# Attention and ternary FFN on one core: the output projection's first tile joins the list between the score rounds, and VectorE masks three of four short rounds

## The reference, cut to what matters

```
xn = layernorm(x)
q, k, v = heads(xn @ Wq.T), heads(xn @ Wk.T), heads(xn @ Wv.T)
q, k = rope(q), rope(k)
attn = softmax(where(causal, q @ k.T / sqrt(32), -inf))
s = (attn @ v) @ Wo.T
h = gelu(layer_norm_quant(xn) @ ternary(w_fc).T)          # 2048 wide
g = silu(layer_norm_quant(h) @ ternary(w_proj).T)
out = x + s * g
```

## Time and profile before

| | us |
|---|---|
| median of 3 runs | 1092.42 |
| lowest and highest run | 1091.6, 1092.45 |
| the profiled execution | 1090.23 |
| its span, first to last instruction | 1088.5 |
| TensorE busy in it | 1062.7 |
| VectorE, ScalarE, GpSimd busy in it | 851.3, 771.9, 551.8 |

### The profile page before, as it was taken

How to read it: one execution, slowest core, us unless ns; L and a number is a source line. 1 busy time by engine, 2 the same in 40 slices (tenths; PEclk the granted TensorE clock), 3 DMA queues, 4 the chain that set the end, 5 groups by cost and what they waited for, 6 DMA issues and landing times.

```text
span 1088.5 us, 19703 instructions
## 1 busy us (share of the span) xinstructions
PE 1062.7 (98%) x7132; PEld 595.4 (55%) x7132; DVE 851.3 (78%) x1751; ACT 771.9 (71%) x1486; POOL 551.8 (51%) x1035
## 2 busy tenths in 40 slices
PE   4999999999999999999999999999999999999998
PEld 3565664448544584446734476444854458444673
DVE  7996877898758986689757997589875898668965
ACT  4797993589826887279853798358982688727984
POOL 2045471565715656265643766156571565626553
PEclk9999999999999999999999999999999999999999
DMA  9493005920129102571027610293012910256101
GB/s 328 166 104 92 1 14 90 118 84 21 38 52 155 40 3 40 80 124 40 4 40 100 104 40 15 57 106 89 22 38 51 156 40 3 40 82 84 40 20 61
DMA packets 87554, 75.66 MB, mean 70 GB/s; under 512 B 44705, under 2 KB 69281, under 8 KB 86945
## 3 DMA queue, kind: packets, MB, share of 16 engines
q1 hardware_dynamic: 87456, 74.41, 37.3%
HBM read 31.98 MB, written 8.40 MB: 37 GB/s over the span
## 4 chain that ended last, share of the span: by engine, by line
PE 80%; ACT 8%; DMA 4%; POOL 4%; DVE 2%; issue 1%; SPq 1%; POOLq 0%; DVEq 0%
PE banks L464 20%; PE banks L601 20%; PE banks L642 16%; PE banks L721 5%; PE banks L481 5%; PE banks L576 4%; PE banks L702 4%; ACT arena L931 3%; DMA norm_row<-norm_c 2%; POOL arena L1500 2%; PE banks L580 2%; ACT banks L911 2%; DMA arena<-in_L_ffn_w_proj_dram 1%; PE banks L587 1%; PE banks L498 1%
## 5 line engine op out<-in xcount | busy, mean ns | idle before, releaser
L911 ACT ACTIVATE banks<-banks,mix,scl 128x384 f32<-128x384 f32 (+2 forms) x384 | 248.6, 650 | 11.8 <-POOL mix L1473 6.1
L642 PE MATMUL banks<-proj_ones,arena 128*128 128x257 f16 (+1 forms) x1792 | 241.7, 272 | 0.0
L601 PE MATMUL banks<-xT,fcT 128*128 128x512 f16 x1024 | 227.7, 379 | 1.9 <-ACT xh_buf L869 1.4
L642 PEld LDWEIGHTS banks<-proj_ones,arena 128*128 128x128 f16 x1792 | 172.9, 97 | 42.3
L1421 POOL TENSOR_TENSOR xh_buf<-xh_buf 128x512 f32<-128x512 f32 x120 | 152.6, 1271 | 66.8 <-ACT xh_buf L869 65.6
L931 ACT ACTIVATE arena<-banks,scl 128x1280 f32<-128x1280 f32 x128 | 163.0, 1331 | 13.2 <-PE banks L702 9.6
L464 PE MATMUL banks<-xT,qkT 128*128 128x512 f16 x768 | 168.1, 379 | 0.1
L601 PEld LDWEIGHTS banks<-xT,fcT 128*128 128x128 f16 x1024 | 99.0, 98 | 122.6 <-ACT xh_buf L869 5.9
L1415 POOL TENSOR_TENSOR xh_buf<-xr_buf,xh_buf 128x512 f16<-128x512 f32 x32 | 36.9, 1175 | 208.8 <-ACT xh_buf L841 208.8
L1211 DVE CUSTOM_DVE_ANT_0 banks<-banks,mask_row 128x512 f32<-128x512 f32 (+1 forms) x224 | 137.7, 632 | 4.3 <-PE banks L576 2.6
L1473 POOL TENSOR_SCALAR mix<-mix,scl 128x1 f32<-128x1 f32 (+1 forms) x288 | 77.1, 268 | 125.8 <-DVE mix L1211 84.6
(11 more groups left out here) (181 smaller groups left out, 1469.2 us busy)
## 6 DMA issues: line engine op xcount, KB each, us to landing
stacks<-xh_buf SPq DMA_DIRECT2D x96, 128.0 KB, 5.5
stacks<-split_buf SPq DMA_DIRECT2D x96, 128.0 KB, 7.9
out_dram<-arena SPq DMA_DIRECT2D x32, 256.0 KB, 2.0
xr_buf<-in_L_attn_x_dram SPq DMA_DIRECT2D x7, 1024.0 KB, 10.1
resid<-in_L_attn_x_dram SPq DMA_DIRECT2D x28, 256.0 KB, 5.3
stacks<-in_L_ffn_w_fc_dram SPq DMA_DIRECT2D x1, 4096.0 KB, 25.7
arena<-in_L_ffn_w_proj_dram SPq DMA_DIRECT2D x1, 4096.0 KB, 15.7
mix<-norm_row SPq DMA_DIRECT2D x8, 256.0 KB, 5.1
```

What stands on the lines that cost most here:

```text
L601: mm = pe.matmul(banks[:, UP_BANKS[f % NUB], :], fcT[:, c, f * P:(f + 1) * P], xT[:, part, c, :], start=(c == 0 and part == 0), stop=(c == ...
L642: mm = pe.matmul(banks[:, DOWN_BANKS[h], 0:cols.stop - cols.start], hid[:, part, f, t * P:(t + 1) * P], proj_ones[:, f, cols], start=(f == ...
L911: mm = nc.scalar.activation(block, block, ACT.Exp, scale=col(EXP_SCALE), bias=exp_bias[:, i, h0 + k:h0 + k + 1], accum_out=row_sum[:, i, h ...
```

## The change

- `OUT_EARLY` goes: all four tiles of the output projection are entries of the running list, 48 instead of 36. `out_projection(b - 1)` ahead of the up-projection goes, and with it the scaling behind chunk 3 and the addition of x there; tile 0 is scaled and added as the others are, at rounds from `SCALED_AFTER`.
- `GIVEN` is planned for 144 entries instead of 132. After rounds 0 to 4 it stays at 0, 4, 12, 17, 20; after round 15 it is 55 instead of 51, after round 26 90 instead of 83, after round 38 128 instead of 118. `SCALED_AFTER` becomes {3: 0, 7: 1, 11: 2, 15: 3} from {3: 1, 7: 2, 11: 3}, `KEEP_DOWN` (19, 25, 29, 35, 39, 43) from (17, 22, 28, 33, 39, 43). `halves_begun(False)` becomes 5 from 6, and `turn_bank_of_half(False)` 6 from 7. For the first example all stays.
- In rounds 15, 26 and 37 of the examples from b = 1 TensorE leaves out the mask product, and VectorE takes each head's maximum with the mask added, in four instructions of 128 columns instead of one of 512.

```diff
+SHORT_WIDE = SHORT[1:]
...
-OUT_EARLY = 1
-OUT_SCALED_AFTER = 3
-OUT_BESIDE_SCORES = (NT - OUT_EARLY) * OUT_MATMULS
+OUT_BESIDE_SCORES = NT * OUT_MATMULS
...
-SCALED_AFTER = {round_behind(GIVEN, (t + 1 - OUT_EARLY) * OUT_MATMULS): t for t in range(OUT_EARLY, NT)}
+SCALED_AFTER = {round_behind(GIVEN, (t + 1) * OUT_MATMULS): t for t in range(NT)}
...
             def out_projection(b):
-                for t in range(OUT_EARLY):
+                for t in range(NT):
                     if t == 0:
                         pe.wait_ge(ctx_lo, b * NG + NG)
-                    three_products(banks[:, 7 - t % 2, :],
-                                   lambda a, r, c: (ctxT[:, a, c, t * P:(t + 1) * P], voT[:, 1, r, c, :]),
-                                   NG, "o").then_inc(wo_ps, 1)
-
-            def late_out_projection(b):
-                for t in range(OUT_EARLY, NT):
                     if t >= 2:
                         pe.wait_ge(scaled_ready, b * NT + t - 1)
...
-                if not first:
-                    out_projection(b - 1)
...
+                    masked_by_dve = r in SHORT_WIDE and not first
                     for k in range(n):
-                        pe.matmul(bank[:, k * keys:(k + 1) * keys], q_stack[0:KS, h0 + k, i * P:(i + 1) * P],
-                                  k_stack[0:KS, h0 + k, 0:keys], start=(k == 0), stop=False)
+                        mm = pe.matmul(bank[:, k * keys:(k + 1) * keys], q_stack[0:KS, h0 + k, i * P:(i + 1) * P],
+                                       k_stack[0:KS, h0 + k, 0:keys], start=(k == 0), stop=(masked_by_dve and k == n - 1))
+                    if masked_by_dve:
+                        mm.then_inc(s_ps, 1)
+                        return
...
-                downs = itertools.chain(() if first else late_out_projection(b - 1), down())
+                downs = itertools.chain(() if first else out_projection(b - 1), down())
...
+                    elif r in SHORT_WIDE and not first:
+                        for k in range(n):
+                            scores = banks[:, S_BANKS[r], k * P:(k + 1) * P]
+                            mm = nc.vector.tensor_tensor_reduce(scores, scores, mask_q, 1.0, MASKED, ALU.add, ALU.max,
+                                                                row_max[:, i, h0 + k:h0 + k + 1])
+                        mm.then_inc(max_ready, 1)
...
-                    if f == OUT_SCALED_AFTER and not first:
-                        scale_by_gate(b - 1, b * 8 + 8, range(OUT_EARLY))
...
-                    if f == OUT_SCALED_AFTER and not first:
-                        for t in range(OUT_EARLY):
-                            add_x(b - 1, t)
```

More of the change, by code:

```diff
@@ L1394, in normalise @@
                     pass
[L1396 to L1400, removed]
             def add_half_of_x(b, t, half):
```

## The result

| | median us | lowest to highest | ratio to before, 95% interval |
|---|---|---|---|
| before | 1092.11 | 1091.6 to 1092.45 | |
| changed | 1110.86 | 1108.65 to 1112.76 | 1.0178 [1.0166, 1.019] |

The change makes the kernel 1.8% slower. The forecast was 1110, range 1100 to 1121. Of the four runs of the changed kernel, 1108.65 and 1109.41 had a mean granted clock of 1.000, and 1112.31 and 1112.76 one of 0.998; the profile is of the first.

What follows compares the result with a forecast made beforehand. TensorE's streaming was taken as the bound; -0.65 -0.13 +1.33 +1.9 = +2.45 us per example, +17 over seven, took 1090.2 to 1107.4, plus 2.2 for the median 1109.6, said as 1110; range 1100 to 1121.

Steps and rivals of the forecast that it cites:

- What bounds: Whole kernel: TensorE streams, busy 1062.7 of 1088.5 us, so a wait entering its queue costs its whole length.
- The rope's cover: Up-projection, chunk 3: TensorE waits for ScalarE's square, held by VectorE's last rope pair; 1.3 us per example.
- The bank: Down-projection half 5, behind round 39's scores: TensorE waits for VectorE's copy out of bank 6, 1.9 us per example.
- The last 2 us of the number: Forecast total: the runs' median lies 2.2 us above the profiled execution, so 1107.4 became 1109.6.
- The 128-wide maxima: Rounds 15, 26, 37 on VectorE: subtraction 1.14 us after the first maximum instead of 0.73; cost 0, up to 0.5.
- Stack landing: Up-projection, chunk 4: square of chunk 1 needs the second stack transfer, landing 337.9; just met, bound 0 to 0.3 us.
- The clock: Rival about TensorE's clock, chance 0.02, no size given; it stays full over a wait of 1.37 us today.
- the masks: Rounds 15, 26 and 37 on TensorE: three mask products go, saving 0.65 us per example in 7 of 8 examples.

Runs made afterwards that it cites:

- masks alone: The kernel before, with only the masks of rounds 15, 26 and 37 moved to VectorE and tile 0 left ahead of the up-projection: 1086.93 us, ratio 0.9958.
- bank 7: The changed kernel with one edit, the begun halves counted as 6 so the turned log-sum's bank stays as before the change: 1095.64 us, ratio 1.0040.
- the move alone: The changed kernel without its masks on VectorE: TensorE adds all masks, only the output projection's tile 0 is moved; 1110.74 us, ratio 1.0179.

## Why the prediction was right

- **What bounds.** TensorE streams, and any wait costs its length: held. The three runs give -0.74 (masks alone) + 1.19 (bank 7 against masks alone) + 1.98 (bank) = +2.43 us per example. Each term is the step from one kernel to the next, so this sum must come out at 131.60 - 129.17 whatever the causes are. A sum that could have failed is the one by stage, from starts in b = 2 of the two kernels. The up-projection's first matmul starts at 333.02 before and 334.29 after, and the first score matmul behind it at

```profile
357.34 0.38 PE L576 MATMUL banks<-stacks 96*128 96x512 f16 x1
...
359.67 0.38 PE L567 MATMUL banks<-stacks 96*128 96x512 f16 x1
```

That is 24.32 and 25.38 us: +1.06. From there to the first exponential behind the rounds (ScalarE, at 405.38 and 411.66) it is 48.04 and 51.99: +3.95, of which 2.59 is the moved tile, -0.65 the three products, and 2.01 is left for the bank. 1.06 - 0.65 + 2.01 = 2.42. Predicted: 1.20 (1.33 - 0.13), -0.65 and 1.9, together 2.45. Seven examples make 17.0 of the span's 18.4; the rest is at the execution's start, where TensorE waited 13.7 us for the weights' maximum instead of 12.1.
- **The rope's cover.** Predicted stall 1.33. Measured: chunk 3 starts 6.38 us after the up-projection, three chunks take 5.18, so 1.20 (a row of 1.04 and the 0.16 that a matmul's row hides). VectorE started chunk 0 4.07 us after the up-projection, predicted 4.17: its next instruction starts 0.07 before the recorded end of the rope (337.14 + 1.29 = 338.43 against 338.36), where the prediction set it 0.02 behind. The 0.13 taken off "at most" came back whole: the 88 matmuls behind the wait take 0.216 each. The runs with 0, 3 and 6 matmuls in front confirm that it is a fixed chain.
- **The bank.** Predicted: copy 1.82 us after round 39's scores start, TensorE at 2.08. Measured 1.77 and 2.12. Put back, 1.98 us return; one place earlier in the queue, 1.1 return.
- **The last 2 us of the number.** The forecast added 2.2 us because the median of the kernel before lay that much above its profiled execution. The median of the changed kernel lies 2.2 us above its own, but by two runs at 0.998 of the clock; the other run at 1.000 is 0.8 above. That 1110 met 1110.86 so closely is in part luck. What the mechanism forecast is the +17.
- **The 128-wide maxima.** Predicted 1.14 us from the first to the subtraction. The chain of the changed kernel, round 37:

```profile
398.43 0.30 DVE banks L1211
...
399.57 0.70 DVE banks L1223
```

399.57 - 398.43 = 1.14, with 0.25 from one to the next of the four. The Trainium skill, VectorE: DVE Perf Modes, section on the TRN2 errata, has (120 + elements) cycles at 0.96 GHz from PSUM to SBUF; for 128 columns that makes an estimate of 0.26 us. The distance from one to the next agrees, the recorded length of one does not: 22.0 us for 84 of them, 0.32 each. The instructions here write PSUM, and the distance also holds 0.06 of the read, so the agreement is a loose one. The page gives its advice against small tiles for sources in SBUF. In kind it is right for VectorE here, which pays 0.4 us per round. That did not decide in rounds 15 to 25, where VectorE had 0.8 us to spare. At round 4, where it has none, it did. Rounds 4 to 14 in the kernel before, same columns as the earlier trace rows:

```profile
364.43:374.52 10.09, 10.09 (x66) 6.05 (x64) 10.09 (x30) 9.59 (x27) 6.08 (x13) 1.00 0.19 68
```

- **Stack landing.** I had it "just met". In the example b = 6 it was not. Timeline of ScalarE there:

```profile
868.37 0.69 ACT L864 ACTIVATE xh_buf<-banks,scl 128x512 f32<-128x512 f32 x1 [0.80 <-DMA stacks<-xh_buf]
```

Square 1 waited 0.80 us for the transfer and the example took 131.9, 0.3 more than the others. ScalarE waits for such a transfer in the profile of every kernel with the move, whole or in part, and in none without it. In all of these but the move alone, TensorE then waits at chunk 4 of one or two examples. So the move brought the landing to the edge of the path, at a cost of 0.3 us in one of seven examples here.
- **The clock.** In the profiled execution it stayed at its full level (mean 1.000) over waits of 1.8 us, seven times. The Trainium skill, TensorE: Matmul & The Clock Gate, Part 1, has idleness lower it; these waits did not. But in two of the four runs the mean granted clock was 0.998, and they are 3 to 4 us longer. The two slowest of the eleven runs with three matmuls in front, 1092.46 and 1093.00, have 0.999 and 0.998 as well. The trace is of a run at 1.000. So whether the clock makes the 4.1 us between the changed kernel's runs, and what lowered it, stays open. The forecast gave the clock 0.02 and was not wrong by it, but it is the one rival that the runs leave standing in part.

What was off is small: inside the changed kernel the masks save 0.27 us per example, not 0.65, mostly because the copy's wait grows with them. The prediction held both numbers (a copy's wait of 1.6 with the old maxima, 1.9 with the new), but never set that growth beside the masks' gain.

## What to carry to other kernels

When work is taken from in front of a stage, list what it covered on the other engines: here twelve matmuls hid the end of the rope; three in front were too few and six enough. When a plan is computed from totals, evaluate every number derived from it before and after; here one count rounding to 5 instead of 6 chose another buffer and cost more than everything else. And time the halves of a change apart: one was worth -0.4%, the other +1.8%.

## What the runs showed of the hardware

A wait of TensorE costs 0.15 to 0.16 us more than the idle time that the trace lists for it: 1.80 is listed and 1.95 lost from start to start at the bank, 1.04 is listed and 1.20 lost at chunk 3. A short loss is not listed at all: 0.25 us in front of round 9 was none, since 0.16 of it lies under the row of the last matmul. Where TensorE looks full, starts of its rows counted against the 0.216 us of a matmul of 512 columns tell more than the list of waits, and so does the other engines' idle time.
